# Row maxima of three attention heads over all 128 partition rows instead of 64, in a two-layer graph network kernel on one Trainium2 core

## What is computed

```python
g = einsum('bcn,bnm->bcm', fea, adj * A_s)
g = relu(g * para)
q = g^T  split into 4 heads of 64
k, v = split(x @ kv_w)
attn = softmax(einsum('bhnd,bhmd->bhnm', q, k) * scale)
out = einsum('bhnm,bhmd->bhnd', attn, v)
x = layernorm(x + out)
```

## Time and profile before

| | us |
|---|---|
| median of three timed runs | 3252.32 (3250.87 to 3254.72) |
| the profiled execution's own time | 3245.61 |
| its span, first to last instruction | 3243.8 |
| TensorE busy (matmul) | 2965.6 (91%) |
| TensorE weight loads | 1830.3 (56%) |
| VectorE busy | 2122.0 (65%) |
| ScalarE busy | 1674.7 (52%) |
| GpSimd busy | 1059.4 (33%) |
| mean granted TensorE clock | 0.970 |

### The profile page before, as it was taken

The page is one execution under the profiler, slowest core; times in us unless marked ns, Lnnn a source line. Parts: engine busy times, 40 slices in busy tenths (PEclk is TensorE's granted clock), DMA queues, the critical chain, the costliest instruction groups (busy, mean ns, idle before and its releaser), DMA issues. The chain is left out here.

```text
span 3243.8 us, 38894 instructions
## 1 busy us (share of the span) xinstructions
PE 2965.6 (91%) x12436; PEld 1830.3 (56%) x12436; DVE 2122.0 (65%) x3015; ACT 1674.7 (52%) x1940; POOL 1059.4 (33%) x500
## 2 busy tenths in 40 slices
PE   6999999999999999999999999999779999997963
PEld 5454555545454554545454554545358888876853
DVE  6677777777677776767777777767453323236877
ACT  5465564646556454646556464655342222226768
POOL 1535244353525344353524435353520000000012
PEclk9999999999999999999999999999989999998986
DMA  4031211213021221303121121302032323225548
GB/s 133 17 117 40 78 58 58 71 46 116 28 89 53 64 61 55 91 26 116 38 79 58 58 65 52 116 17 74 14 123 78 113 81 108 86 91 202 194 158 282
DMA packets 168269, 276.13 MB, mean 85 GB/s; under 512 B 9760, under 2 KB 109088, under 8 KB 168224
## 3 DMA queue, kind: packets, MB, share of 16 engines
q1 hardware_dynamic: 168224, 275.55, 26.7%
HBM read 174.60 MB, written 67.11 MB: 75 GB/s over the span
## 5 line engine op out<-in xcount | busy, mean ns | idle before, releaser
L261 POOL TENSOR_TENSOR psum<-psum,probs 128x1024 f32<-128x1024 f32 x320 | 813.8, 2543 | 245.4 <-ACT probs L326 235.9
L326 ACT ACTIVATE probs<-sc_ps 128x1024 f32<-128x1024 f32 x512 | 523.9, 1023 | 682.7 <-PE sc_ps L791 681.3
L504 DVE TENSOR_REDUCE mx<-mx_ps 128x1 f32<-128x512 f32 x768 | 492.9, 684 | 196.8 <-PE mx_ps L759 194.6
L807 PE MATMUL pv_ps<-probs,v 128*64 128x512 f32 x2048 | 550.0, 615 | 2.8 <-ACT probs L326 2.6
L791 PE MATMUL sc_ps<-qa,ka 128*128 128x512 f32 x1024 | 448.1, 446 | 0.0
L791 PE MATMUL sc_ps<-qb,kb 128*128 128x512 f32 x1024 | 403.7, 399 | 0.0
L261 POOL TENSOR_TENSOR psum<-probs 128x1024 f32<-128x1024 f32 x64 | 152.1, 2377 | 700.7 <-ACT probs L326 378.4
L791 PEld LDWEIGHTS sc_ps<-qa,ka 128*128 128x128 f32 x1024 | 194.0, 191 | 289.8 <-issue 173.8
L759 PE MATMUL mx_ps<-ka,qa 64*128 64x512 f32 x768 | 296.5, 452 | 12.7 <-DVE xT_lo L458 3.7
L723 PE MATMUL sc_ps<-w_hi,x_hi 128*128 128x512 f32 x512 | 211.8, 414 | 44.3 <-DVE w_lo L471 44.3
L759 PEld LDWEIGHTS mx_ps<-ka,qa 64*128 64x128 f32 x768 | 119.0, 184 | 233.8 <-DVE mx L504 138.4
(11 more groups left out here) (182 smaller groups left out, 5271.0 us busy)
## 6 DMA issues: line engine op xcount, KB each, us to landing
adj_ring<-in_adj_dram SPq DMA_DIRECT2D x128, 512.0 KB, 3.9
pre_scratch<-pre SPq DMA_DIRECT2D x32, 1024.0 KB, 4.2
hid<-pre_scratch SPq DMA_DIRECT2D x32, 1024.0 KB, 5.1
x<-in_x_dram SPq DMA_DIRECT2D x16, 1024.0 KB, 7.3
kb<-ka SPq DMA_DIRECT2D x64, 256.0 KB, 3.1
qa<-qa SPq DMA_DIRECT2D x64, 256.0 KB, 3.3
res<-in_x_dram SPq DMA_DIRECT2D x16, 1024.0 KB, 5.6
x_scratch<-res SPq DMA_DIRECT2D x16, 1024.0 KB, 4.3
```

The lines of the kernel that those rows point to most:

```text
L261: pool.tensor_tensor(psum[:, :], probs[:, 0, :] if k == 1 else psum[:, :], probs[:, k % PR, :], ALU.add).then_inc(s["pool_added"], 1)
L326: nc.scalar.activation(probs[:, i % PR, :], sc_ps[:, t % 2, :], ACT.Exp, scale=SCALE)\
L504: nc.vector.tensor_reduce(mx2[:, nh, n:n + 1], mx_ps[:, nh, :], AX.X, ALU.max)\
L807: ins = nc.tensor.matmul(pv_ps[nh * HD:(nh + 1) * HD, h % 2, :], v[:, i, h * HD:(h + 1) * HD], probs[:, i % PR, nh * BANK:(nh + 1) * BANK] ...
```

## The change

The maxima of heads 1 to 3 are computed from all 128 rows of `qa[h]` and `ka[h]` instead of the head's own 64, so from q_hi times (k_hi + k_lo). Number, shape and place of the matmuls stay; so do head 0's maxima, VectorE's reductions and the merge of the halves with one operand. Since the other rows are read now, the first of them in a head waits for the copy of `qa` (`qa_in`) and for k's trailing part (`kl_done`) where it waited for `qh_done`.

```diff
@@ max_scores
                 elif n == 0:
                     wait(pe, s["row_done"], 4 * b + h)
-                    wait(pe, s["qh_done"], 4 * b + h + 1)
+                    wait(pe, qa_in[h], 16 * (b + 1))
+                    wait(pe, s["kl_done"], 4 * b + h + 1)
                     if h == 1:
                         wait(pe, s["v_evac"], 2 * b + 2)
...
                     out = mx_ps[:, nh, :] if h else sc_ps[:, n % 2, nh * BANK:(nh + 1) * BANK]
-                    nc.tensor.matmul(out, qa[h][own(h), n * P:(n + 1) * P], ka[h][own(h), nh * BANK:(nh + 1) * BANK],
+                    rows = slice(0, P) if h else own(h)
+                    nc.tensor.matmul(out, qa[h][rows, n * P:(n + 1) * P], ka[h][rows, nh * BANK:(nh + 1) * BANK],
                                      start=True, stop=True).then_inc(s["mx_ready"], 1)
```

## The result

| | before | after |
|---|---|---|
| median of the timed runs, us | 3253.52 (3250.87 to 3261.07) | 3213.93 (3213.04 to 3214.61) |
| ratio, 95% interval | | 0.9879 [0.9863, 0.9895] |
| the profiled execution's own time, us | 3245.61 | 3214.61 |
| span, us | 3243.8 | 3212.8 |
| mean granted clock | 0.970 | 0.968 |

The change makes the kernel faster by 1.2%, 39.6 us by the medians. The forecast was 3219 us, in a range of 3195 to 3239.

The account below looks back on a forecast made before the run. TensorE was taken to set the pace, VectorE next at 72%. Five two-pair places at 0.15 and seven pairs at 0.19 gave 2.08 us a batch, 33 us over 16 batches: 3252.3 - 33 = 3219 us, range 3195 to 3239.

Parts of the forecast that it names:

- The price of a pair, 0.19 us: Between scores and values on TensorE, a pair over 128 rows saves one shape change: 0.66 - 0.47 = 0.19 us.
- Where VectorE holds: Pairs waiting for VectorE's reductions gain less or nothing, leaving 2.08 us a batch, 33 us, instead of 73.
- The five two-pair places: Two pairs with only scores between them: VectorE holds the second, so each place gives 0.15 us, not 0.38.
- the held places: Pairs already waiting before the change, such as n = 0 and 1 of heads 1 and 3: they give nothing.
- pairs n = 5 in heads 2 and 3: Four transposes stand between pairs 5 and 6, leaving VectorE enough time, so each gives 0.19 us.
- Rival 1: Full gain: VectorE doesn't hold any pair, so 73 us are won, 3179 us; chance 0.07.
- n = 7 of head 2: Its 0.19 us is lost ahead of head 3's first pair, which waits on GpSimd additions, q_low and xt_low.
- Rival 3: Slower: VectorE and GpSimd collide in a new place, 2.4 us a batch lost, 3257 us or 3296; chance 0.05.
- The waits: The added waits on qa_in and kl_done cost nothing, being for old events; at most 5 us if not hidden.
- Rival 2: No gain: weight loads over 128 rows aren't hidden, matmuls start 0.33 us apart, 3252 us; chance 0.08.
- The clock, taken as no change: Clock dips in the batch periods stay as they are; at the ends some 8 us won or 5 lost.

Follow-up runs that it names:

- the mixed pairs: The changed kernel with the second matmul of each pair over 64 rows again, the first still over 128: 3267.18 us, ratio 1.0036.
- the waits-alone kernel: The kernel before with only the new waits (qa_in, kl_done) in place of qh_done, maxima still over 64 rows: 3249.25 us, ratio 0.9968.
- the one with the collision: The changed kernel with maxima 2 and 3 placed later and q_low of head 3 moved behind its first three maxima: 3237.71 us, ratio 0.9952.

## Why the prediction was right

**The price of a pair, 0.19 us.** Right: 0.98 became 0.78 us. That it is a price for changing the array's shape was an argument; the mixed pairs show it.

**Where VectorE holds.** Right place by place, as the table shows. The five two-pair places gave 0.12 to 0.15 us each where 0.15 was said, the held places nothing. The sum came to 1.95 us a batch where 2.08 was forecast; the terms that were a little too large are the 0.19 of pairs n = 5 in heads 2 and 3, which run into transposes (0.34 and 0.35 for n = 5 and 6 together, not 0.38), and the 0.15 that were 0.12 to 0.14. Rival 1, the full gain of 73 us, is out for this kernel; with VectorE's reductions cut in half it is come near to, 61 us by the periods.

**n = 7 of head 2.** Right: the 0.19 us won there are lost again in front of head 3, and they come back when one q_low is taken out of the chain: the idle time of 0.38 us and more there is gone. **Rival 3**, a new collision of VectorE and GpSimd, isn't seen in the changed kernel: the long q_low, that of head 3, takes 3.28 us as it took 3.29 before, and the two engines' busy times stand within 0.5 us a period.

**The waits.** Right: nothing, by the period of 143.54 us.

**Rival 2, the load that isn't hidden.** Out: pairs over 128 rows follow the scores at 0.23 us, and each other where neither VectorE nor a change of shape is in the way. The Trainium skill (TensorE: Matmul & The Clock Gate, Part 3) has loads overlap matmuls only when the row group differs, though the same part also lets a load go ahead of running matmuls when it targets the background weight buffer. Here nearly every load of the attention layer is over 128 rows (head 0's maxima are not), and its busy time stands beside the matmuls', not behind it (second and third number, of 2267.13 us), so the measurement decides against the first sentence:

```profile
36.67:2303.80 2267.13, 2149.65 (x8988) 1215.68 (x8988) 1649.01 (x2353) 1274.95 (x1369) 1001.03 (x414) 0.99 0.21 65
```

**The clock, taken as no change.** This step is the one that failed, by 8 us. The sum gave 33 us and the periods gave 31, but the medians moved by 39.6. The timed runs of before in all groups spread from 3244 to 3269 us; the four of the changed kernel stay within 1.6 us. The profiled execution of before (3245.6 us) was near its fast end, and the waits-alone kernel shows a program with the same full-clock period 10 us longer at a lower clock, with 9 of 14 periods dipped instead of 6 (five with one dip, four with two). So some 8 us of the timed gain are dips that before has in its typical run over those of its profiled execution. The changed kernel isn't free of them: its profiled execution, 0.7 us above its median, has them in 9 of 14 periods, but only one period has two. The bounds given for the clock (8 us won, 5 lost) just held it, and that is luck in part, for they were reckoned from dips that would all go or come in the profiled execution, and there they about cancel. (The 8 us themselves fit the trace of before, though it has four periods with one dip and two with two, not half of all and two deeper.) What sets how many dips an execution gets wasn't settled.

## What to carry to other kernels

Price a matmul by the spacing of starts around it, not by its busy time: here the changed group got no shorter and the kernel got 31 us shorter, with dips of the clock that cost about the same in both traces. A small product that uses half the rows between full products may cost less over all rows, since every change of shape has its price. Then look who waits for whom at the place where time is won: half of it was lost to reductions that became the bound, and two moves in the order of that engine gave back 28 us, nearly as much again.

## What the runs showed that I had not expected

- The clock differs from version to version as well as from one execution to the next. The order of maxima that shortened each full-clock period by 0.37 us had a profiled span 7 us longer, with a mean clock of 0.964 instead of 0.968. The kernel before with q_low moved had a dip in every period of its profiled execution. That the length of the period is the cause isn't shown: at one and the same full-clock length, the kernel before and the waits-alone kernel had 6 and 9 periods with dips.
- A dip from 2.4 to 1.2 GHz costs 0.8 us in the kernel before where a period holds one (143.54 against 144.37), some 0.65 in the changed one, and 2.3 us where it holds two and shows 0.98 (141.55 against 143.83). Of all kernels but the one with the collision, the dips of the loop fall at two places in the batch, from 0.4 us before to 1.6 us after the end of a wait of TensorE. One is the wait of 2.0 us for head 0's maxima; the other is in the graph product, a wait of 1.15 us for w_low and then one of 1.75 us for the last addition to the sums of head 3 (`add_last`), here in the kernel before; the last two rows start 0.43 us apart instead of 0.23, so the clock has fallen:

```profile
1186.66 0.50 PE L723 MATMUL sc_ps<-w_hi,x_hi 128*128 128x512 f32 x1 [1.15 <-DVE w_lo L471]
...
1190.07 1.08 PE L817 MATMUL pv_ps<-psum,ones_a 128*64 128x512 f32 x4 [1.75 <-DVE psum L521]
...
1191.43 0.63 PE L723 MATMUL sc_ps<-w_hi,x_lo 128*128 128x512 f32 x1
1191.86 0.63 PE L723 MATMUL sc_ps<-w_lo,x_hi 128*128 128x512 f32 x1
```

- Differences of 10 us between runs of one program (3245 us at clock 0.969 and 3255 at 0.966 in the waits-alone kernel) go with the clock. Full-clock periods of one trace agree within 0.2 us, some 3 us of the launch, and so tell versions apart that the medians don't.
